# A graph layer's histogram and edge sums: one-hots with the chunk as the last index, and units of seven chunks

## The chip, the cores and the metric

The kernel runs on one core of a Trainium2 chip. Its five engines work side by side and meet through semaphores: PE (TensorE, matmuls and, as PEld, the loads of their weights), DVE (VectorE), ACT (ScalarE), POOL (GpSimd, which here issues gathers) and SP (SyncE, which issues the other transfers). The metric is the device time of one execution in microseconds.

## The reference

The input is a graph of N = 6250 nodes and E = 100000 edges, whose edges are sorted by destination, with a row of 512 numbers for each node. Four blocks follow one another, each added to its input:

```python
x = x + _L0_gnn_ref(_layernorm(x), node_vec1, W1, b1, gamma, beta, W2, b2, edge_index)   # A, B and part of C
x = x + _L0_ffn_ref(_layernorm(x)[None], w_gate, w_up, w_down)[0]                        # C
x = x + _L1_gnn_ref(_layernorm(x), edge_index, 6250, alpha, W, b)                        # D
x = x + _L1_ffn_ref(_layernorm(x)[None], switch_w, switch_b, expert_w, expert_b)[0]      # D and the last stage
...
deg = jax.ops.segment_sum(jnp.ones_like(src, dtype=x.dtype), dst, num_segments=N)   # first block, with self loops
h = x @ W1                                            # 512 -> 8
...
agg = jax.ops.segment_sum(x[src], dst, num_segments=num_nodes)                      # third block: rows of 512
agg = agg / jnp.maximum(deg, 1.0)[:, None]
return x + alpha * (agg @ W.T + b)
```

Two things matter here: the degree of each node, which is a histogram of the destinations, and the third block's sum of 512 numbers over the edges of each destination.

## The kernel before

The nodes lie in NT = 49 tiles of P = 128, the edges in C = 784 chunks of 128. The program has five stages, one behind the other, with a barrier of all engines between two: A (degrees and x @ W1), B (first edge sum and the quantized weights), C (second edge sum and the feed-forward block), D (third block and routing) and the experts. The change touches A and D, and one step of B.

**Stage A.** SP brings in the two edge lists and the rows of x. DVE turns the lists into numbers with an edge for each partition (`dstT`, `srcT`; PE does the transposes, DVE copies each of 14 blocks out of `pL`), finds for each chunk the first and the last tile and for each tile its range of chunks (lines 484 to 530, among them `pres`, `span`, `row` and `low_b`), and splits the destinations into `lo_f` (low 7 bits) and `hiT_f` (tile). Then a loop of G = 7 rounds runs on DVE, ACT and PE at once, each with its own order written out by hand:

- DVE: statistics of seven tiles of x (line 551), two histogram batches, the six small steps of the scales (`newton`, line 563), six more batches. A batch covers HU = 14 chunks: line 537 writes `ol`, 14 one-hots of 128 low ids, and line 540 `oh`, 14 one-hots of 49 tiles, each compared as f32 and written as bf16, laid out chunk by chunk. Two batches are buffered (`hist_used`).
- ACT: the scaled rows (`norm`, line 589) and the copies of the turned rows (line 603).
- PE: per batch 14 matmuls (line 653), with one chunk of `ol` as the 128 by 128 weights and the same chunk of `oh` as 49 columns, summed in `pD`; per tile four transposes (`turn`, line 636) and four matmuls with W1 (`layer1`, line 645), whose weights are the turned rows in f32.

The buffer `xt` of x holds one round, so the statistics of a round start when its loads are in. At the end DVE forms the degrees, `hid` and its split parts (lines 569 to 580), which SP stores.

**Stage D.** The chunks are grouped in CQ units of Q = 4. POOL gathers, chunk by chunk, rows of 1024 f16 numbers into a ring of RING = 7 units (line 1611). It waits for room in the ring (`rows_used`, counted up by DVE at line 1890) and, AHEAD = 3 units later, for the unit's arrival, which it passes on as `rows_ready` (line 1605). A unit is visited once for each tile that its edges reach. In a visit DVE builds the one-hots of the unit against that tile (line 1884, 512 numbers for each partition) and adds the sum of the visit before into `agg` (line 1872); PE multiplies each chunk's one-hot with both halves of its rows (line 1711, 2 Q matmuls of 512 columns) into one of two banks `pV`. Loops over units and visits have counts read from the tables `units` and `counts`, which stage B computes; at each unit's end PE and DVE read the next entry into a register. Behind a tile's units PE turns it (line 1728), multiplies it with W (1736, 1738) and computes the logits of a tile of the round before (1746, 1756). The rows of the tables are read at lines 1520 (`counts`) and 1523 (`units`).

## Time and profile before

| | us |
|---|---|
| median of three runs | 3950.85 |
| lowest and highest | 3946.94, 3951.02 |
| the profiled execution | 3950.55 |
| its span, first to last instruction | 3948.8 |
| stage A, up to the first work of stage B | 312.3 |
| its loop of seven rounds (43.0 to 293.5) | 250.5 |
| stage D, first gather to last (2417.7 to 3562) | about 1144 |

A timeline row gives the start, the duration, the engine, the line, the operation with its operands and how many instructions were merged; in brackets stands the idle time of the engine before it and what released it, where "issue" means that nothing in the profile was waited for. In a group's row the mean is that of one instruction.

### The profile page before, as it was taken

Reading aid. Unit: us, or ns where it says so; the run is one execution under the profiler, and the core shown is the slowest. Engines: PE = TensorE matmul, PEld = TensorE weight load, DVE = VectorE, ACT = ScalarE, POOL = GpSimd, SP = SyncE. Lnnn points to the kernel's source line nnn. Section 1 sums busy time; section 2 is a strip of 40 time slices with the busy share of each in tenths; the row PEclk is TensorE's granted clock in tenths of the full one; section 3 lists DMA queues with packets and bytes.
Section 4 is the critical chain, followed back from the end, with each engine's and each line's share of the span. In section 5 each row is a group of like instructions: output and inputs, shape, how many; then the busy total and the mean of one; then the engine's idle time right before and its main releaser. Section 6 shows DMA issues by size and latency. Waiting matters only on the chain. (4 is left out here: it accounts for less than half of the span.)

```text
span 3948.8 us, 60722 instructions
## 1 busy us (share of the span) xinstructions
PE 2807.3 (71%) x16139; PEld 2048.0 (52%) x16140; DVE 2086.5 (53%) x3745; ACT 1053.4 (27%) x1677; POOL 2087.1 (53%) x2184
## 2 busy tenths in 40 slices
PE   3664556320399999999999994677666676766599
PEld 3564555320277777777777883223232232323487
DVE  7777888992345454545454434443434434343476
ACT  1234446200123232323232331011111121213344
POOL 0006777775777777777500003776656665660254
PEclk9998778655599999999999997999999999997699
DMA  1113224102023333333322324777666666762464
GB/s 53 48 39 59 53 46 110 15 5 37 4 65 108 84 100 84 102 82 106 83 97 83 101 89 149 221 234 215 191 205 201 201 206 184 220 196 81 141 212 132
DMA packets 249317, 458.11 MB, mean 116 GB/s; under 512 B 93442, under 2 KB 115058, under 8 KB 249094
## 3 DMA queue, kind: packets, MB, share of 16 engines
q0 software_dynamic: 112384, 235.97, 23.1%
q1 hardware_dynamic: 136710, 219.40, 17.3%
q8 instruction: 111, 1.82, 0.2%
q14 instruction: 112, 0.92, 0.1%
HBM read 388.49 MB, written 73.25 MB: 117 GB/s over the span
## 5 line engine op out<-in xcount | busy, mean ns | idle before, releaser
L1611 POOL DMA_INDIRECT rows<-xn_rows,srcT x784 | 741.1, 945 | 403.6 <-issue 216.3
L115 POOL DMA_INDIRECT msg_c<-hid_rows,srcT x784 | 758.2, 967 | 251.2 <-issue 232.8
L1711 PE MATMUL pV<-rows,oh 128*128 x1952 | 474.1, 387 | 241.2 <-DVE agg L1872 193.8
L115 POOL DMA_INDIRECT msg_b<-hid_rows,srcT x464 | 455.7, 982 | 148.5 <-issue 137.2
L1711 PEld LDWEIGHTS pV<-rows,oh 128*128 x1952 | 190.6, 98 | 511.5 <-issue 356.9
L1273 PE MATMUL acc<-wd,hT 128*128 128x512 f32 x1617 | 414.8, 405 | 3.1 <-issue 1.2
L1248 PE MATMUL pG<-xT,wgu_hi 128*128 128x512 f32 (+1 forms) x1232 | 371.1, 382 | 22.9 <-issue 21.3
L1248 PE MATMUL pU<-xT,wgu_hi 128*128 128x512 f32 (+1 forms) x1232 | 364.2, 377 | 13.2 <-DVE sil L1417 13.2
L1884 DVE SCALAR_TENSOR_TENSOR oh<-ids,bases,dstT 128x512 f32 x244 | 183.2, 751 | 357.0 <-issue 322.7
L1273 PEld LDWEIGHTS acc<-wd,hT 128*128 128x128 f32 x1617 | 306.9, 193 | 77.4 <-issue 13.8
L1872 DVE TENSOR_TENSOR agg<-agg,pV x245 | 167.8, 685 | 269.2 <-PE pV L1711 257.8
L1248 PEld LDWEIGHTS pG<-xT,wgu_hi 128*128 128x128 f32 x1232 | 232.0, 193 | 67.6 <-issue 35.2
L1248 PEld LDWEIGHTS pU<-xT,wgu_hi 128*128 128x128 f32 x1232 | 230.3, 192 | 49.6 <-issue 22.3
L1038 PE MATMUL pG<-parts,los 128*128 128x200 bf16 x1920 | 220.9, 286 | 43.4 <-DVEq L874 24.7
L1597 POOL IOTA bases<- 128x49 f32 x1 | 0.2, 180 | 465.5 <-POOLq L334 465.5
L1736 PE MATMUL pW<-wgT,aT 128*128 128x512 f32 x392 | 211.2, 689 | 46.8 <-DVEq L1906 46.8
L1038 PEld LDWEIGHTS pG<-parts,los 128*128 128x128 bf16 x1920 | 201.5, 114 | 61.0 <-ACT los L1006 26.2
L1248 PE MATMUL pG<-xT,wgu_lo 128*128 128x512 f32 (+1 forms) x616 | 229.6, 373 | 0.0
L1248 PE MATMUL pU<-xT,wgu_lo 128*128 128x512 f32 (+1 forms) x616 | 228.7, 371 | 0.0
L1417 DVE TENSOR_TENSOR sil<-pU,sil 128x512 f32<-128x512 f32 (+1 forms) x154 | 95.8, 622 | 248.9 <-PE pU L1248 241.2
L1794 ACT ACTIVATE wg<-agg,invdeg 128x512 f32 (+1 forms) x49 | 35.3, 721 | 659.1 <-DVEq L104 659.1
L1325 ACT ACTIVATE sil<-pG 128x512 f32<-128x512 f32 (+1 forms) x154 | 84.0, 545 | 444.3 <-PE pG L1248 441.2
(362 smaller groups left out, 4625.9 us busy)
## 6 DMA issues: line engine op xcount, KB each, us to landing
wd<-wd_rows SPq DMA_DIRECT2D x154, 512.0 KB
we<-in_L_ffn_expert_w SPq DMA_DIRECT2D x16, 1024.0 KB, 8.0
msg_c<-hid_rows,srcT POOLq DMA_INDIRECT x784
x_rows<-xr SPq DMA_DIRECT2D x49, 256.0 KB, 4.1
xn_rows<-pair SPq DMA_DIRECT2D x49, 256.0 KB
rows<-xn_rows,srcT POOLq DMA_INDIRECT x784
res<-x_rows SPq DMA_DIRECT2D x49, 256.0 KB, 3.9
x_rows<-agg SPq DMA_DIRECT2D x49, 256.0 KB, 2.9
```

What stands on the lines that cost most here:

```text
L115: nc.gpsimd.indirect_dma_start(msg[:, c, :], None, table, bass.IndirectOffsetOnAxis(ap=srcT[:, c:c + 1], axis=0)).then_inc(landed[u % 2], 16)
L1038: last = nc.tensor.matmul(into, los[:, g % 2, b, k * P:(k + 1) * P], parts[:, j, b].rearrange("p f h -> p (f h)"), start=(b == 0 and j == ...
L1248: last = nc.tensor.matmul(ps[:, 0:n], w[:, c, :], v[:, c, :], start=(m == 0), stop=(m == len(terms) - 1))
L1273: last = nc.tensor.matmul(acc4[j][:], h, wd[:, slot, w, :], start=(f == 0 and m == 0), stop=(f == FB - 1 and m == 2))
L1325: nc.scalar.activation(sil[:, 0:n], pG[:, 0:n], ACT.Silu).then_inc(s["silu"], 1)
L1417: nc.vector.tensor_tensor(sil[:, 0:n], pU[:, 0:n], sil[:, 0:n], ALU.mult).then_inc(s["hmul"], 1)
L1611: nc.gpsimd.indirect_dma_start(rows[:, u % RING, c, :], None, xn2_rows, bass.IndirectOffsetOnAxis(ap=srcT[:, u * Q + c:u * Q + c + 1], axi ...
L1711: last = nc.tensor.matmul(pV[:, ds(to, 1), :].rearrange("p a d -> p (a d)"), oh[:, ds(of, 1), c, :].rearrange("p a d -> p (a d)"), rows[:, ...
L1736: nc.tensor.matmul(pW[:], aT[:, k % 2, c, :], wgT[:, c, :], start=(c == 0), stop=False)
L1794: nc.scalar.activation(scaled[:, k % 2, :], agg_at(T), ACT.Identity, scale=invdeg[:, ds(T, 1)]).then_inc(s["scaled"], 1)
L1872: nc.vector.tensor_tensor(at, at, pV[:, ds((v + 1) % 2, 1), :].rearrange("p a b -> p (a b)"), ALU.add).then_inc(s["added"], 1)
L1884: nc.vector.scalar_tensor_tensor(oh[:, ds(v % 4, 1)].rearrange("p a q n -> p (a q) n"), bc(ids.unsqueeze(1), (P, Q, P)), bases[:, ds(tile, ...
```

## The change

Constants: units of seven chunks in place of four, a ring of four units in place of seven (28 chunks both times), and the wait for a unit's arrival after the fourth gather of the unit behind it. Stage A: the lists are loaded in two parts, the first of which waits for nothing, and destinations first; `xt`, `var`, `mv` and `rs` are doubled; the one-hots are bf16 comparisons of a constant table `number` with `lo_b` and `hi_b`, four batches deep, laid out with the chunk as the last index; the list blocks are turned four and three at a time; and the rounds are written out, with the statistics and scales of the next round between the batches of this one, and the work on the tile ranges between the batches of the first. Stage B: the tile's last unit is found by a multiplication and a shift. Stage D: `landed` and `oh3` have two buffers each.

```diff
-Q = 4
+Q = 7
 CQ = C // Q
+BY_Q = -(-(1 << 16) // Q)
+assert CQ * Q == C and all(n * BY_Q >> 16 == n // Q for n in range(C))
...
-RING = 7
-BY_R = -(-(1 << 16) // 7)
+RING = 4
+BY_R = -(-(1 << 16) // RING)
 assert all(n * BY_R >> 16 == n // RING for n in range(256))
-AHEAD = 3
+LANDING = 4
...
-            ol = sb(ctx, "ol", [P, 2, HU, P], BF16)
-            oh = sb(ctx, "oh", [P, 2, HU, NT], BF16)
+            HB = 4
+            ol = sb(ctx, "ol", [P, HB, P, HU], BF16)
+            oh = sb(ctx, "oh", [P, HB, NT, HU], BF16)
+            number = sb(ctx, "number_a", [P, P, HU], BF16)
...
-                sp.dma_start(w1[:], W1.rearrange("(k p) h -> p k h", p=P)).then_inc(s["w1_in"], 16)
...
+                EA = 96
+                lists = ((dst, dst_em, "dst_in"), (src, src_em, "src_in"))
+                for lst, em, done in lists:
+                    sp.dma_start(em[0:EA, :], lst[0:EA * EB * P].rearrange("(p c) -> p c", p=EA)).then_inc(s[done], 16)
                 sp.wait_ge(s["cleared"], 2)
...
-                def load(i, k, rows=P):
-                    sp.dma_start(xt[0:rows, k, :], x[ds((i * G + k) * P, rows), :]).then_inc(x_in[k], 16)
+                def load(i, k):
+                    if i >= 2:
+                        sp.wait_ge(s["xT_ps"], (i - 2) * G + k + 1)
...
+                sp.dma_start(w1[:], W1.rearrange("(k p) h -> p k h", p=P)).then_inc(s["w1_in"], 16)
...
+                def histogram(i, m):
+                    n = i * HG + m
+                    if n >= HB:
+                        dve.wait_ge(s["hist_used"], n - HB + 1)
+                    nc.vector.tensor_tensor(ol[:, n % HB], number[:], bc(lo_b[:, n * HU:(n + 1) * HU].unsqueeze(1), (P, P, HU)),
+                                            ALU.is_equal).then_inc(s["ol"], 1)
+                    nc.vector.tensor_tensor(oh[:, n % HB], number[:, 0:NT], bc(hi_b[:, n * HU:(n + 1) * HU].unsqueeze(1), (P, NT, HU)),
+                                            ALU.is_equal).then_inc(s["oh"], 1)
...
+                first = {1: extreme_tiles, 2: lambda: turned_list(2), 3: lambda: turned_list(3), 4: spans, 6: span_rows, 7: tile_ranges}
...
+                nc.vector.memset(dst_em[96:EP, :], FAR).then_inc(s["cleared"], 1)
+                nc.vector.memset(src_em[96:EP, :], 0).then_inc(s["cleared"], 1)
...
-                def histogram(i, m):
-
-                    n, h = i * HG + m, m % 2
-
-                    dve.wait_ge(s["hist_used"], n + 1)
-                    nc.vector.tensor_tensor(
-                        ol[:, h, :, :], bc(iota[:].unsqueeze(1), (P, HU, P)),
-                        bc(lo_f[:, ds(n * HU, HU)].unsqueeze(2), (P, HU, P)), ALU.is_equal).then_inc(s["ol"], 1)
-                    nc.vector.tensor_tensor(
-                        oh[:, h, :, :], bc(iota[:, 0:NT].unsqueeze(1), (P, HU, NT)),
-                        bc(hiT_f[:, ds(n * HU, HU)].unsqueeze(2), (P, HU, NT)), ALU.is_equal).then_inc(s["oh"], 1)
...
-                with dve.Fori(0, G) as i:
-                    own.body(i, 3 + NEWTON)
-
-                    dve.wait_ge(s["xn"], i * G + G)
-                    for k in range(G):
-                        dve.wait_ge(x_in[k], (i + 1) * 16)
-                        last = nc.vector.bn_stats(st[:, k, :], xt[:, k, :])
-                    own.step(last)
...
-                    nc.vector.tensor_copy(sig[:, 0:1], var[:, 0:1]).then_inc(s["var"], 1)
-                    for m in range(2):
...
+                statistics(0, range(G))
+                variance(0)
+                for i in range(G):
+                    for m in range(HG):
                         histogram(i, m)
-                    dve.wait_ge(s["std"], i + 1)
-                    newton(nc, own, rs[:, :, 0], var[:], nw[:])
-                    nc.vector.scalar_tensor_tensor(rs[:, :, 1], mv[:, :, 0], -1.0, rs[:, :, 0],
-                                                   ALU.mult, ALU.mult).then_inc(s["stats"], 1)
-                    for m in range(2, HG):
-                        histogram(i, m)
-                own.end(G)
+                        if i == 0 and m == 0:
+                            scales(0)
+                        if i == 0 and m in first:
+                            first[m]()
+                        if i == 1 and m == 0:
+                            low_ids()
+                        if i + 1 < G:
+                            if m < 4:
+                                statistics(i + 1, range(2 * m, min(2 * m + 2, G)))
+                            if m == 4:
+                                variance(i + 1)
+                            if m == 6:
+                                scales(i + 1)
...
-                nc.vector.tensor_copy(sig[:, 0:1], degs[:, 0:1]).then_inc(s["degs"], 1)
...
-                own.step(nc.vector.tensor_scalar_max(invdeg[:], pD[:, 0:NT], 1.0))
-                own.step(nc.vector.reciprocal(invdeg[:], invdeg[:]))
-
-                dve.wait_ge(s["h_used"], G + 1)
+                dve.wait_ge(s["h_used"], G)
...
                 split3(nc, own, own3, hid, hrest)
                 dve.sem_inc(s["hid1"], 1)
+                own.step(nc.vector.tensor_scalar_max(invdeg[:], pD[:, 0:NT], 1.0))
+                own.step(nc.vector.reciprocal(invdeg[:], invdeg[:]))
...
                 def turn(i, k):
-                    pe.wait_ge(s["xn"], i * G + (k + G + 1))
+                    T = i * G + k
+                    pe.wait_ge(s["xn"], T + 1)
+                    if T >= 2:
+                        pe.wait_ge(s["xT"], T - 1)
                     for c in range(DK):
-                        last = nc.tensor.transpose(pT[k % 2][:, c * P:(c + 1) * P], xt[:, k, c * P:(c + 1) * P], ident[:])
+                        last = nc.tensor.transpose(pT[T % 2][:, c * P:(c + 1) * P], xt[:, i % 2, k, c * P:(c + 1) * P], ident[:])
                     last.then_inc(s["xT_ps"], 1)
 
...
                 def histogram(i, m):
-                    pe.wait_ge(s["ol"], i * HG + (m + 1))
-                    pe.wait_ge(s["oh"], i * HG + (m + 1))
+                    n = i * HG + m
+                    pe.wait_ge(s["ol"], n + 1)
+                    pe.wait_ge(s["oh"], n + 1)
                     for c in range(HU):
-                        last = nc.tensor.matmul(pD[:, 0:NT], ol[:, m % 2, c, :], oh[:, m % 2, c, :], start=False, stop=False)
+                        last = nc.tensor.matmul(pD[:, 0:NT], ol[:, n % HB, :, c], oh[:, n % HB, :, c], start=False, stop=False)
                     last.then_inc(s["hist_used"], 1)
 
-                with pe.Fori(0, G) as i:
-                    histogram(i, 0)
-                    histogram(i, 1)
-                    turn(i, 0)
-                    for k in range(G):
-                        if k + 1 < G:
-                            turn(i, k + 1)
-                        layer1(i, k)
-                        if k % 2 == 0:
-                            histogram(i, 2 + k // 2)
-                    for m in range(2 + -(-G // 2), HG):
+                for i in range(G):
+                    for m in range(HG):
                         histogram(i, m)
+                        if i == 0 and m in first:
+                            first[m]()
+                        if m < G:
+                            turn(i, m)
+                        if m > 0:
+                            layer1(i, m - 1)
                 nc.tensor.matmul(pD[:, 0:NT], identb[:], zeros[:], start=False, stop=True).then_inc(s["hist"], 1)
...
+                own.step(nc.vector.tensor_scalar_mul(v[1], v[1], float(BY_Q)))
                 own.step(nc.vector.tensor_copy(ti[0:1, 0, :], v[1]))
-                own.step(nc.vector.tensor_single_scalar(ti[0:1, 1, :], ti[0:1, 0, :], Q.bit_length() - 1, ALU.arith_shift_right))
+                own.step(nc.vector.tensor_single_scalar(ti[0:1, 1, :], ti[0:1, 0, :], 16, ALU.arith_shift_right))
...
-        landed = [sem(f"d_landed{h}") for h in range(AHEAD + 1)]
+        landed = [sem(f"d_landed{h}") for h in range(2)]
...
-            oh = sb(ctx, "oh3", [P, 4, Q, P], F16)
+            oh = sb(ctx, "oh3", [P, 2, Q, P], F16)
...
                 def arrived(u):
-                    pool.wait_ge(landed[u % (AHEAD + 1)], (u // (AHEAD + 1) + 1) * Q * 16)
+                    pool.wait_ge(landed[u % 2], (u // 2 + 1) * Q * 16)
                     pool.sem_inc(s["rows_ready"], 1)
 
...
-                    if u >= AHEAD:
-                        arrived(u - AHEAD)
-                for u in range(CQ - AHEAD, CQ):
-                    arrived(u)
+                            bass.IndirectOffsetOnAxis(ap=srcT[:, u * Q + c:u * Q + c + 1], axis=0)).then_inc(landed[u % 2], 16)
+                        if c + 1 == LANDING and u > 0:
+                            arrived(u - 1)
+                arrived(CQ - 1)
...
-                            to, of = v % 2, v % 4
+                            to = v % 2
...
-                                        oh[:, ds(of, 1), c, :].rearrange("p a d -> p (a d)"),
+                                        oh[:, ds(to, 1), c, :].rearrange("p a d -> p (a d)"),
...
-                            wait_alone(dve, s["mm_done"], v + 1, s["fence_dve"])
                             nc.vector.scalar_tensor_tensor(
-                                oh[:, ds(v % 4, 1)].rearrange("p a q n -> p (a q) n"), bc(ids.unsqueeze(1), (P, Q, P)), bases[:, ds(tile, 1)],
+                                oh[:, ds(v % 2, 1)].rearrange("p a q n -> p (a q) n"), bc(ids.unsqueeze(1), (P, Q, P)), bases[:, ds(tile, 1)],
```

PE, stage A, in one of the seven rounds; `pT` holds turned rows, `pH` the product with W1, `pD` the histogram. Before, the loop's start:

```order
L653 MATMUL pD<-oh,ol 128x49 x14
L650 REGISTER_ALU
L653 MATMUL pD<-oh,ol 128x49 x14
L634 ISA
L636 MATMUL pT<-ident,xt 128x128 x4
L634 REGISTER_ALU
L636 MATMUL pT<-ident,xt 128x128 x4
L642 REGISTER_ALU
L643 REGISTER_ALU
L645 MATMUL pH<-w,xT 128x8 x4
L650 REGISTER_ALU
```

Now, the second round:

```order
L709 MATMUL pD<-oh,ol 128x49 x14
L689 MATMUL pT<-ident,xt 128x128 x4
L709 MATMUL pD<-oh,ol 128x49 x14
L689 MATMUL pT<-ident,xt 128x128 x4
L700 MATMUL pH<-w,xT 128x8 x4
L709 MATMUL pD<-oh,ol 128x49 x14
L689 MATMUL pT<-ident,xt 128x128 x4
```

A batch of 14 stands ahead of each tile's transposes, and the product of a tile one batch behind its transposes, in place of two batches at the start and two or three at the end.

DVE, stage A, from the statistics of a round to its second batch. Before:

```order
L551 BN_STATS st<-xt 128x6 x7
L94 ISA
L555 BN_AGGR mv<-st 128x2 x7
L94 REGISTER_ALU
L557 TENSOR_SCALAR var<-mv 128x7
L94 REGISTER_ALU
L558 COPY sig<-var 128x1
L536 REGISTER_ALU
L537 ISA
L537 TENSOR_TENSOR ol<-iota,lo_f 128x1792
L540 REGISTER_ALU
L540 TENSOR_TENSOR oh<-iota,hiT_f 128x686
```

Now, in the second round:

```order
L492 BN_STATS st<-xt 128x6
L521 TENSOR_TENSOR ol<-number_a,lo_b 128x1792
L523 TENSOR_TENSOR oh<-number_a,hi_b 128x686
L499 BN_AGGR mv<-st 128x2 x7
L501 TENSOR_SCALAR var<-mv 128x7
L521 TENSOR_TENSOR ol<-number_a,lo_b 128x1792
L523 TENSOR_TENSOR oh<-number_a,hi_b 128x686
L521 TENSOR_TENSOR ol<-number_a,lo_b 128x1792
L523 TENSOR_TENSOR oh<-number_a,hi_b 128x686
L2219 RECIPROCAL rs<-rs 128x7
L2220 TENSOR_TENSOR nw<-var,rs 128x7
```

The statistics stand between the batches, two tiles at a time, and belong to the next round.

PE, stage D, the end of a unit: the last matmul, the two loop ends and the reading of the next unit. Before:

```order
L1711 ISA
L1711 MATMUL pV<-rows,oh 128x512
L1717 ISA
L1704 COMPARE_AND_BRANCH
L1718 ISA
L1523 TENSOR_LOAD units
L1523 ISA x2
L1688 ISA
L1698 COMPARE_AND_BRANCH
```

Now:

```order
L1764 ISA
L1764 MATMUL pV<-rows,oh 128x512
L1770 ISA
L1757 COMPARE_AND_BRANCH
L1771 ISA
L1577 TENSOR_LOAD units
L1577 ISA x2
L1741 ISA
L1751 COMPARE_AND_BRANCH
```

The same rows end a unit; ahead of them stand 14 matmuls in a visit in place of 8, each with one ISA row that sets an address.

## Rows read from the trace of the kernel before

**Rows 1.** window, then us and instructions of PE, PEld, DVE, ACT, POOL, clock, DMA.

```profile
43.00:293.50 250.50, 158.50 (x1358) 153.84 (x1358) 197.53 (x266) 74.07 (x118) 0.00 (x0) 1.00 0.15 45
...
2416.60:3562.00 1145.40, 768.08 (x3078) 342.77 (x3078) 482.66 (x853) 183.44 (x271) 741.74 (x788) 0.93 0.70 208
```

**Rows 2.** timeline of DVE, stage A: start, us, line, operation, idle before and its releaser.

```profile
18.72 0.63 DVE L481 CAST dst_f<-dst_em 112x896 f32<-112x896 int32 x1 [15.90 <-DMA dst_em<-in_dst]
...
19.80 0.62 DVE L484 TENSOR_SCALAR hi_i<-dst_em 112x896 int32<-112x896 int32 x1
...
27.79 1.02 DVE L504 CAST dstT<-pL 128x112 int16<-128x112 f32 x2
...
37.97 0.27 DVE L514 TENSOR_REDUCE spanr<-pL 98x1 f32<-98x112 f32 x1
...
42.92 4.25 DVE L551 BATCH_NORM_STATS2 st<-xt 128x6 f32<-128x512 f32 x7 [0.44 <-DVE low_b L530]
...
48.35 2.03 DVE L537 TENSOR_TENSOR ol<-iota,lo_f 128x1792 bf16<-128x1792 f32 x1
50.30 0.87 DVE L540 TENSOR_TENSOR oh<-iota,hiT_f 128x686 bf16<-128x686 f32 x1
51.08 2.02 DVE L537 TENSOR_TENSOR ol<-iota,lo_f 128x1792 bf16<-128x1792 f32 x1
```

**Rows 3.** timeline of PE, first round of stage A.

```profile
51.31 0.74 PE L653 MATMUL pD<-oh,ol 128*128 128x49 bf16 x14 [12.65 <-DVE oh L540]
...
59.43 0.75 PE L653 MATMUL pD<-oh,ol 128*128 128x49 bf16 x14
59.99 1.09 PE L636 MATMUL pT<-ident,xt 128*128 128x128 f32 x4
...
62.45 1.09 PE L636 MATMUL pT<-ident,xt 128*128 128x128 f32 x4
```

**Rows 4.** groups by line: operation, count | busy us, mean ns | idle us before, releasers.

```profile
L1711 PEld LDWEIGHTS pV<-rows,oh 128*128 x1952 | 190.6, 98 | 511.5 <-issue 356.9
...
L537 DVE TENSOR_TENSOR ol<-iota,lo_f 128x1792 bf16<-128x1792 f32 x56 | 113.3, 2023 | 50.3 <-PE pD L653 49.6
...
L645 PEld LDWEIGHTS pH<-w,xT 128*128 128x128 f32 x392 | 88.5, 333 | 1.5 <-ACT xT L603 1.5
...
L540 DVE TENSOR_TENSOR oh<-iota,hiT_f 128x686 bf16<-128x686 f32 x56 | 48.5, 867 | 0.0
...
L1962 DVE TENSOR_TENSOR names<-names,iota 128x448 bf16<-128x448 bf16 x7 | 4.4, 625 | 0.7
...
L1963 DVE TENSOR_SCALAR names<-names,lane 128x448 bf16<-128x448 bf16 x7 | 2.5, 352 | 0.2
```

**Rows 5.** timeline of DVE where the loop of stage A ends.

```profile
294.45 0.21 DVE L569 TENSOR_SCALAR degs<-pD 128x49 f32<-128x49 f32 x1 [0.97 <-PE pD L668]
```

**Rows 6.** timeline of PE, stage D, around one tile.

```profile
3002.64 1.90 PE L1711 MATMUL pV<-rows,oh 128*128 x8 [1.92 <-DVE agg L1872]
3006.25 1.90 PE L1711 MATMUL pV<-rows,oh 128*128 x8 [1.72 <-DVE agg L1872]
3008.54 1.90 PE L1711 MATMUL pV<-rows,oh 128*128 x8 [0.39 <-issue]
3012.11 0.63 PE L1728 MATMUL pT<-ident,wg 128*128 128x128 f32 x4 [1.67 <-issue]
```

**Rows 7.** timeline of PE, stage D, second visit of another tile.

```profile
3215.20 1.90 PE L1711 MATMUL pV<-rows,oh 128*128 x8 [0.91 <-issue]
```

**Rows 8.** timeline of DVE, stage D, beside Rows 6.

```profile
3003.89 0.75 DVE L1884 SCALAR_TENSOR_TENSOR oh<-ids,bases,dstT 128x512 f32 x1 [1.39 <-issue]
3005.07 0.69 DVE L1872 TENSOR_TENSOR agg<-agg,pV  x1 [0.43 <-issue]
```

**Rows 9.** gathers on POOL: the group, and one row of its timeline.

```profile
L1611 POOL DMA_INDIRECT rows<-xn_rows,srcT x784 | 741.1, 945 | 403.6 <-issue 216.3 <-DVEq L1890 186.4 <-DMA rows<-xn_rows,srcT 0.9
...
3013.41 0.94 POOL L1611 DMA_INDIRECT rows<-xn_rows,srcT  x1 [0.30 <-issue]
```

More of the change, by code:

```diff
@@ L374, in program @@
             "dve lists_f lists_ps lists_used lo_hi ol oh hist_used hist "
-            "span var std degs degs_std fence span_ps spanr row_ps ranges lows pool hid1 stored ".split())}
-        x_in = [sem(f"a_x_in{k}") for k in range(G)]
+            "span var std degs degs_std span_ps spanr row_ps ranges lows numbers pool hid1 stored ".split())}
+        x_in = [[sem(f"a_x_in{j}_{k}") for k in range(G)] for j in range(2)]
         with ExitStack() as ctx:
@@ L472, in _ @@
                 nc.gpsimd.memset(dstT[:, C:DX], FAR).then_inc(s["const"], 1)
+                nc.gpsimd.iota(number[:], [[1, P], [0, HU]], base=0, channel_multiplier=0,
+                               allow_small_or_imprecise_dtypes=True).then_inc(s["numbers"], 1)
             @block.vector
@@ L476, in _, with statistics @@
                 own = Steps(dve, s["dve"])
-                nc.vector.memset(src_em[:], 0).then_inc(s["cleared"], 1)
-                nc.vector.memset(dst_em[:], FAR).then_inc(s["cleared"], 1)
-                dve.wait_ge(s["dst_in"], 32)
+                def statistics(i, ks):
+                    for k in ks:
+                        dve.wait_ge(x_in[i % 2][k], (i // 2 + 1) * 16)
+                        last = nc.vector.bn_stats(st[:, k, :], xt[:, i % 2, k, :])
+                    own.step(last)
@@ L501, in _ @@
[L501 to L506 removed]
+                turned_list(0)
+                turned_list(1)
+                dve.wait_ge(s["lists_used"], 2)
@@ new lines, in turn_list, with spans @@
+                    last.then_inc(s["lists_ps"], 1)
+                for j in range(4):
+                    turn_list(j) if j < 2 else None
+                nc.tensor.matmul(pD[:, 0:NT], identb[:], zeros[:], start=True, stop=False)
+                def spans():
+                    pe.wait_ge(s["span"], 1)
+                    pe.wait_ge(s["lists_used"], 4)
+                    nc.tensor.transpose(pL[0][0:2 * NT, 0:EP], span[:].rearrange("p a b -> p (a b)"),
+                                        ident[0:EP, 0:EP]).then_inc(s["span_ps"], 1)
```

212 lines of the change are left out of this document (118 added, 94 removed).

## The prediction

> **What bounds the kernel now.** I read the windows by stage first, then the timelines of two stages. A barrier stands between the stages, so that a microsecond saved in a stage is saved in the whole, and only A and D change much. The loop of stage A takes 250.5 us, and no engine is busy for all of it: DVE for 197.5 and PE for 158.5 [rows 1]. The reader is to see why in the timelines: each round begins with the statistics of seven tiles, in which PE has nothing to do, and later DVE waits for one of its two buffers, which PE frees late (50.3 us over the loop, [rows 4]). A round takes 250.5 / 7 = 35.8 us. Before it stand 42.9 us in which DVE prepares the lists [rows 2]. The granted clock is 1.00 in the loop, which is the level of 2.4 GHz.
>
> Stage D could be taken as bound by its gathers. POOL starts one every 1.25 us (0.94 us and 0.30 before it, [rows 9]), which for 784 is 980 us of 1145. But POOL also stands 186.4 us behind DVEq L1890, the count that frees the ring [rows 9]: it is held back by the consumers. Of these PE is the later one. Its visits last 1.90 us. From a unit's last visit to the next start 3.61 us pass, inside a unit 3.61 - 1.71 + 0.39 = 2.29 [rows 6]. The gap of 1.7 us is attributed to `agg`, but the same 1.67 stands before the transposes at L1728, which don't read `agg` and whose releaser is "issue" [rows 6]. So it belongs to the end of a unit: loop ends and the load of the next table entry. The table load and the branches are rows of the program's order that don't change.
>
> **Stage A, start.** The first batch reaches PE at 51.3 us [rows 3]. Of DVE's work ahead of it these leave: the first and last tiles and their spans, 27.79 - 19.80 = 8.0 us; the tile ranges and low ids, 42.92 - 37.97 = 5.0 us [rows 2]. They come back in the first round (12 us) and the second (about 1 us). Of the 14 list copies, 10.2 us from 27.79 to 37.97 with the five conversions, the seven of src move too and the other seven become two; I put list and conversions at 2.5 + 3.0 us, an estimate from the five conversions in those 10.2 us and the copies' rows. The destinations arrived at 18.7 us, last in their queue; now they are first, and most of the list doesn't wait for the memsets. If that brings nothing, PE starts at 18.7 + 1.2 (casts) + 5.5 + 5.4 (statistics, from 42.92 to 48.35) + 1.4 = 32.2 us; if it brings 9 us, at 23. I take 28.
>
> **Stage A, DVE's round.** One batch costs DVE 1.95 us for `ol` and 0.78 for `oh`, start to start [rows 2]. The difference of 1.17 us for 1106 numbers is 1.06 ns each, with 0.05 us fixed. All operands are now bf16 and dense. The case shows no such comparison: a bf16 multiplication with one f32 operand, 625 ns for 448 numbers, has no gain; with no f32 stream, 352 ns, it does [rows 4]. So the new cost lies between nothing gained (2.73 us a batch) and half for each number (1.00 + 0.42 = 1.42). I take 1.42, since the second row differs from the first in just what the change makes different. The Trainium skill, "VectorE: DVE Perf Modes", section "The perf-mode tier table", gives two-operand bf16 instructions in SBUF twice the rate; no row of this case shows it for two streams. A round is then 8 x 1.42 + 5.4 (statistics) + 1.2 (six small steps of about 0.2, as in [rows 5]) = 18.0 us, against 28.4 without the gain.
>
> **Stage A, PE's round.** A tile's four transposes and four products take 62.45 - 59.99 = 2.46 us; a batch of 14 takes 59.99 - 59.43 = 0.56 us, or 40 ns a matmul [rows 3]. The four buffers and the statistics of the next round ahead of time let PE go on from batch to tile, and ACT's copies and scalings have the whole round for seven tiles, so that nothing but PE's own work is on the path. At the old price a round is 7 x 2.46 + 8 x 0.56 = 21.7 us. But PE now reads both operands with a step of 14 numbers, 28 bytes. No row shows a strided read. The lower end is 40 ns. The upper end is the nearest row of a slow weight load, f32 weights at 333 ns each [rows 4]: 7 x 2.46 + 112 x 0.333 = 54.5 us. Between them lies a bf16 load that nothing overlaps, 98 ns on average at L1711 [rows 4], and I take this, 112 x 0.098 + 17.2 = 28.2 us: if reads get slower, the overlap that makes 98 ns into 40 is what goes first.
>
> The Trainium skill has a rule on either side. "SBUF — State Buffer", section "Door 1: The DMA port swizzle", says that reads run at full rate while successive accesses fall on the same line of 16 bytes, and pay for each new line; by it every one of these reads pays, which speaks against the change. "TensorE: Matmul & The Clock Gate", section "Weight-path perf modes — Fast Weight Load (FWL) and DoubleRow", keeps the fast load for 128 bf16 weights at such a step. By the second the round would be the 21.7 us of the rival below, by the first alone more. No run here shows either yet.
>
> **Stage A, sum.** The first round has DVE's 18.0 + 12.4 = 30.4 us, more than PE's 28.2; six rounds follow at 28.2: 28 + 30.4 + 169.2 = 227.6 us. Before, the loop ended at 293.5 (PE's last matmul released DVE at 294.45, [rows 5]). Saved: 65.9, and 0.9 more since the two `invdeg` steps move behind `hid1`, behind which SP's store and the barrier wait. That is 67. The iota of `number` on POOL (1792 numbers for each partition) is over long before 20 us. SP's loads wait for a tile of two rounds earlier and have no one behind them who is late.
>
> **Stage B.** One small step more, and about a dozen on a row of 162 in place of 246: nothing, within 1 us. They stand on DVE ahead of the tiles' loop.
>
> **Stage D.** From the inputs: 196 units and 244 visits become 112 units and, with 48 tile borders, 160 visits; matmuls rise from 1952 to 2240. A visit of 14 at 1.90 / 8 = 0.2375 us is 3.33 us. Before: 196 x 3.61 + 48 x 2.29 = 817 us. Now, if the gap at a unit's end stays: 112 x (3.33 + 1.71) + 48 x (3.33 + 0.39) = 743 us. Saved: 74. The gap may also shrink: where PE's sequencer had run ahead it was 0.91 [rows 7], and longer matmuls hide more of the issue. Then DVE's chain bounds a unit: sum of the visit before (0.53 us after its end, 0.69 long), 1.39 of issue, the one-hot at 0.75 + 384 x 1.04 ns = 1.15, and some 0.7 to PE's start, 4.5 to 4.6 us [rows 6, 8]. 112 x 4.6 + 48 x 3.5 = 683 us would save 134. I take 74, since three of four gaps at a unit's end in [rows 6, 7] are the long ones. DVE's added 0.4 us in a visit lies beside 3.33 us of PE, its summations fall by 84 beside PE as well; the removed wait on `mm_done` had been met two visits before.
>
> The ring holds 28 chunks as before, but is freed by the unit: POOL may run some 14 to 21 chunks ahead instead of 20 to 24. With 1145 - 74 = 1071 us for 980 us of gathers that should do. A unit is announced four gathers, 5 us, behind its last one instead of 15.
>
> **The sum.** 3950.55 - 67 - 74 = 3809.6 us, against the profiled execution's own time, which is 0.3 us below the median of the three runs.
>
> **Rivals.** (1) *Strided reads cost nothing*: a round of 21.7, A saves 105 + 1, 3950.55 - 106 - 74 = 3770 us. For it: weights go in faster than numbers one by one already. (2) *Strided reads are the new bound, and slower*: at the f32 price the loop ends at 28 + 7 x 54.5 = 410 us, A loses 115, 3950.55 + 115 - 74 = 3992 us. It decides from 28 + 7 x (17.2 + 112 p) = 368, p = 0.28 us a matmul. For it: each column is its own access for both operands. Against it: that is seven times the dense price. (3) *Stage D gains nothing*: with two units ready, a tile's 8 us of other work, or the ten-us stall of POOL once a round, empties the ring, or landing takes over 5 us; 3950.55 - 67 = 3884 us. (4) *The comparisons don't speed up*: DVE's 28.4 us bound the round, first round 40.8, end at 29 + 40.8 + 170.4 = 240, A saves 54, 3823 us.
>
> **How the numbers follow.** Forecast 0.40, rival 1 0.34, rival 2 0.07, rival 3 0.12, rival 4 0.07. The predicted time is the forecast's, 3810 us. The range goes down to rival 1 with D's better bound, 3950.55 - 106 - 130 = 3715, and up to rival 3, 3885; rival 2 stays out. A measurement of this kernel can tell about 0.2%. Faster by more 0.92, within it 0.01, slower 0.07.
>
> **What would show it.** Right: line 521 near 1.05 us; the first PE batch before 33 us; a batch of 14 in about 1.4 us, rounds of 28 us without idle time on PE; in D units 5.0 us apart, POOL's wait for the ring down to about 110 us. Wrong: a batch of 14 on PE at 0.6 us or at 4; PE waiting for POOLq in D; line 521 still at 2.0 us.

## The result, and the profile after

The changed kernel takes 3727.68 us, the median of four runs (3721.67 to 3729.46), against 3950.85 before: a ratio of 0.9435, with an interval of 0.9418 to 0.9451. Its profiled execution has a span of 3726.1 us, 222.7 us less than before. Of the kernels below, `d_alone` had one run of four at a lower granted clock, 4492.61 us at 0.653 in place of 0.89, which its numbers leave out. By stage, from the first gather of one to that of the next:

| us | before | after | saved | forecast |
|---|---|---|---|---|
| A, up to B's first gather | 313.5 | 242.3 | 71.2 | 67 |
| B | 628.7 | 626.6 | 2.1 | 0 |
| C | 1475.5 | 1466.3 | 9.2 | 0 |
| D, first gather to the last matmul of the sums | 1173.6 | 1039.9 | 133.7 | 74 |
| D, from there to the experts' first matmul | 118.5 | 112.6 | 5.9 | 0 |
| experts | 239.0 | 238.4 | 0.6 | 0 |

The windows of stages A and D after, in the columns of [rows 1]:

```profile
23.70:223.30 199.60, 194.35 (x1382) 193.00 (x1382) 130.93 (x268) 65.62 (x111) 0.00 (x0) 1.00 0.16 48
2334.00:3360.00 1026.00, 821.46 (x3394) 375.50 (x3394) 434.54 (x696) 184.19 (x272) 743.56 (x788) 0.92 0.77 232
```

In A, PE is busy for 194 of 199.6 us, where it was for 158 of 250; DVE has time to spare. In D the clock and the gathers' count are as before, in 1026 us instead of 1145.

Stage A starts earlier. The timeline of DVE, which stands beside [rows 2]:

```profile
22.06 1.09 DVE L521 TENSOR_TENSOR ol<-number_a,lo_b 128x1792 bf16<-128x1792 bf16 x1
23.07 0.51 DVE L523 TENSOR_TENSOR oh<-number_a,hi_b 128x686 bf16<-128x686 bf16 x1
23.50 0.20 DVE L2219 RECIPROCAL rs<-rs 128x7 f32<-128x7 f32 x1
```

`ol` costs 1.01 us and `oh` 0.43, start to start, in place of 1.95 and 0.78. PE's first batch starts at 23.73 us in place of 51.3. PE in the second round, beside [rows 3]:

```profile
64.57 1.48 PE L709 MATMUL pD<-oh,ol 128*128 128x49 bf16 x14
65.88 1.05 PE L689 MATMUL pT<-ident,xt 128*128 128x128 f32 x4
66.72 1.72 PE L700 MATMUL pH<-w,xT 128*128 128x8 f32 x8
68.29 1.48 PE L709 MATMUL pD<-oh,ol 128*128 128x49 bf16 x14
```

From 61 us on no idle time is left, a tile's transposes and products take 68.29 - 65.88 = 2.41 us (2.46 before), and a batch of 14 takes 65.88 - 64.57 = 1.31 us (1.29 to 1.32 elsewhere) in place of 0.56. Stage D around three tiles, beside [rows 6]:

```profile
2908.55 3.19 PE L1764 MATMUL pV<-rows,oh 128*128 x14
2912.57 6.27 PE L1764 MATMUL pV<-rows,oh 128*128 x28 [0.83 <-issue]
2920.10 0.63 PE L1781 MATMUL pT<-ident,wg 128*128 128x128 f32 x4 [1.27 <-issue]
...
2949.96 3.19 PE L1764 MATMUL pV<-rows,oh 128*128 x14 [0.67 <-issue]
2954.44 5.84 PE L1764 MATMUL pV<-rows,oh 128*128 x26 [1.29 <-DVE agg L1925]
```

Visits of 14 matmuls take 3.19 us, and the gaps between units 0.67 to 1.29 us instead of 1.7. A unit whose edges reach two tiles is visited twice, and these two visits follow each other with no gap (28 matmuls in one row, cut at 26 by the window's edge in the last). The groups of D's sums and of its gathers, beside [rows 4, 9]:

```profile
L1665 POOL DMA_INDIRECT rows<-xn_rows,srcT x784 | 743.2, 948 | 282.2 <-issue 244.4 <-DVEq L1942 23.6 <-DMA rows<-xn_rows,srcT 14.2
L1764 PE MATMUL pV<-rows,oh 128*128 x2240 | 528.8, 392 | 94.5 <-issue 44.9 <-DVE agg L1925 38.9 <-DVE oh L1936 10.3
```

POOL waits 23.6 us for room in the ring, where it waited 186.4; 743.2 + 282.2 us cover the stage, and 244.4 of the idle time is "issue", most of it the 0.30 us between two gathers: issuing the gathers is now nearly all of it.

### The profile page after: what moved, and what is told of

Its sections match the earlier page's. It is cut to its first block and busy times, and to the rows that moved or that the text cites. A ratio compares the mean times of both kernels' runs of the same rounds, so it can differ in the third digit from the quotient of the medians.

```text
span 3726.1 us, 57890 instructions
## 1 busy us (share of the span) xinstructions
PE 2878.9 (77%) x16427; PEld 2109.9 (57%) x16428; DVE 1957.7 (53%) x3559; ACT 1045.3 (28%) x1671; POOL 2091.5 (56%) x2185
## 5 line engine op out<-in xcount | busy, mean ns | idle before, releaser
L1665 POOL DMA_INDIRECT rows<-xn_rows,srcT x784 | 743.2, 948 | 282.2 <-issue 244.4
L1764 PE MATMUL pV<-rows,oh 128*128 x2240 | 528.8, 392 | 94.5 <-issue 44.9
L1764 PEld LDWEIGHTS pV<-rows,oh 128*128 x2240 | 223.2, 100 | 387.7 <-issue 180.1
L1936 DVE SCALAR_TENSOR_TENSOR oh<-ids,bases,dstT 128x896 f32 x160 | 184.1, 1151 | 210.7 <-issue 210.5
L1925 DVE TENSOR_TENSOR agg<-agg,pV x161 | 110.1, 684 | 336.6 <-PE pV L1764 335.2
L1386 ACT CAST hT<-sil 128x512 fp32r<-128x512 f32 (+1 forms) x154 | 87.3, 567 | 405.9 <-DVE sil L1471 404.6
```

The lines of the kernel that those rows point to most:

```text
L1386: nc.scalar.copy(hT[:, slot, 0, 0:n], sil[:, 0:n]).then_inc(s["h_hi"], 1)
L1665: nc.gpsimd.indirect_dma_start(rows[:, u % RING, c, :], None, xn2_rows, bass.IndirectOffsetOnAxis(ap=srcT[:, u * Q + c:u * Q + c + 1], axi ...
L1764: last = nc.tensor.matmul(pV[:, ds(to, 1), :].rearrange("p a d -> p (a d)"), oh[:, ds(to, 1), c, :].rearrange("p a d -> p (a d)"), rows[:, ...
L1925: nc.vector.tensor_tensor(at, at, pV[:, ds((v + 1) % 2, 1), :].rearrange("p a b -> p (a b)"), ALU.add).then_inc(s["added"], 1)
L1936: nc.vector.scalar_tensor_tensor(oh[:, ds(v % 2, 1)].rearrange("p a q n -> p (a q) n"), bc(ids.unsqueeze(1), (P, Q, P)), bases[:, ds(tile, ...
```

## Experiments

Six kernels change the one-hots of stage A, three change D (two of them were run twice), and one changes only the length of PE's program. Each is quoted with what was written before it ran.

**The stages apart.** `d_only` takes the parts of B and D into the kernel before, as in the diff ahead; `d_q4` takes units of four into the kernel after:

```diff
-Q = 7
+Q = 4
...
-RING = 4
+RING = 7
```

> The kernel before with the changes of stages B and D alone (units of seven, ring of four, arrival after the fourth gather, two one-hot buffers, no wait on mm_done); stage A stays as before. From the profile after: first gather of stage D to its last matmul 1039.9 us against 1173.6 before, and 5.9 us less from there to the experts. Theory (the stages' gains are separate, and D gives 134 to 140 us): 3950.9 - 140 = 3811 us, stage A up to the first gather of stage B 313 us as before. Rival (stage C's 9.2 us, which came for no reason that the change shows, hang on the layout of memory that stage D's smaller tables bring): 3802, with stage C at 1466 in place of 1475 us. Second rival (D gained because stage A left something different): D above 1060, over 3835 us.

> The kernel after with units of four and a ring of seven again, all else kept (arrival passed on after the fourth gather of the next unit, two one-hot buffers, no wait on mm_done in DVE). Theory (what was gained in D is the fixed price of a unit's end on PE, which 84 units fewer don't pay and longer visits hide): D back at 1165 to 1185 us from first gather to last matmul, gaps of 1.6 to 1.8 us between the visits of two units, total 3727.7 + 135 = 3863 us (3845 to 3880). Rival (the removed wait of DVE or the earlier announcement did it): D below 1100, total under 3790 us.

Both told nothing about D: where they ran, every kernel was slow, and the kernel before took 5713 us. `d_only` took 5660 us and `d_q4` 5640. The gathers of D in `d_only`:

```profile
L1614 POOL DMA_INDIRECT rows<-xn_rows,srcT x784 | 746.5, 952 | 656.2 <-DVEq L1891 410.8 <-issue 227.8 <-DMA rows<-xn_rows,srcT 17.5
```

POOL waits 410.8 us for the ring, so it is held back by the consumers. They hardly wait for the gathers: the time that PE and its weight loads stood idle at D's sums is put to "issue" for 812.1 us (854 times; in the kernel after 225.0, 279 times) and to the units' arrival for 10.1. The expectation of `d_q4_again` below blames the gathers, which these numbers don't bear out; what slowed these kernels stays open. Stage A, which has no gathers, took 313.5 us in `d_only` and 241.9 in `d_q4`, as expected. The same two kernels ran again, beside a kernel before of 3949.9 us:

> The same kernel as d_only (before, with the changes of stages B and D alone). Theory (the stages are separate): first gather to last matmul 1040 us, total 3951 - 134 - 6 = 3811 us. If stage C's 9 us come with the tables of stage D: 3802.

`d_alone` took 3807.7 us, the median of three (ratio 0.9652, 0.9633 to 0.9671), with 1037.9 us from first gather to last matmul and stage C at 1475.0. The stages are separate, and C's 9 us don't come from D.

> The same kernel as d_q4 (after, with units of four and a ring of seven). In the first comparison every kernel's gathers were slow, the kernel before's too, so that stage D stood on them in all kernels. Where gathers take 1.25 us each again: theory (the fixed price of a unit's end on PE): first gather to last matmul 1165 to 1185 us, total 3863 us (3845 to 3880). Rival (DVE's removed wait or the earlier announcement brought it): under 1100 us, total under 3790.

`d_q4_again` took 3856.8 us (0.9767, 0.9751 to 0.9783), with 1174.8 us in D, what the kernel before has. All that D gained comes from the size of the unit; with units of four, the removed wait of DVE, the two buffers and the earlier announcement bring nothing that can be seen. PE in it, in the columns of [rows 6]:

```profile
2918.72 1.90 PE L1764 MATMUL pV<-rows,oh 128*128 x8 [1.68 <-DVE agg L1925]
2920.91 1.90 PE L1764 MATMUL pV<-rows,oh 128*128 x8 [0.29 <-issue]
2924.49 0.63 PE L1781 MATMUL pT<-ident,wg 128*128 128x128 f32 x4 [1.68 <-issue]
```

The gap behind a unit is 1.68 us again. It stands before a visit and before the transposes alike.

**What the gap is.** `d_split` leaves the columns as they are and doubles the instructions:

```diff
-for m in range(2):
+for m in range(4):
...
-pV[:, ds(to, 1), :].rearrange("p a d -> p (a d)"),
+pV[:, ds(to, 1), m % 2 * 256:m % 2 * 256 + 256].rearrange("p a d -> p (a d)"),
...
-rows[:, ds(at, 1), c, m * D:(m + 1) * D].rearrange("p a d -> p (a d)"),
-start=(c == 0 and m == 0), stop=(c == Q - 1 and m == 1))
+rows[:, ds(at, 1), c, m * 256:m * 256 + 256].rearrange("p a d -> p (a d)"),
+start=(c == 0 and m == 0), stop=(c == Q - 1 and m == 3))
```

> The kernel after with each matmul of stage D's sums of 512 columns issued as two of 256: 28 instructions a visit in place of 14, the same columns. Theory (PE's sequencer bounds a unit: from consecutive visits of two units, 3.61 us with 8 matmuls and 4.48 with 14, each matmul costs it 0.145 us and a unit's end 2.45): a unit takes 2.45 + 28 x 0.145 = 6.5 us in place of 4.5, and a visit inside a unit 4.1 + 0.6 = 4.7; stage D's sums 112 x 6.5 + 48 x 4.7 = 954 us with about 340 us of other work on PE, first gather to last matmul near 1300 us. Rival (the gap at a unit's end is a fixed wait behind the array's last matmul, whatever the count of instructions): 1040 to 1070 us.

Measured: 1249.8 us in D, 3952.4 in all (3941.2 to 3963.4). The rival falls. PE's timeline:

```profile
2904.42 3.22 PE L1764 MATMUL pV<-rows,oh 128*128 x28
2908.99 3.95 PE L1764 MATMUL pV<-rows,oh 128*128 x28 [1.35 <-DVE agg L1925]
2913.92 3.97 PE L1764 MATMUL pV<-rows,oh 128*128 x28 [0.98 <-issue]
2920.18 0.73 PE L1781 MATMUL pT<-ident,wg 128*128 128x128 f32 x4 [2.30 <-issue]
```

The first visit behind other work takes 3.22 us, near the 3.19 of 14 matmuls: its 28 instructions had been handed over while the tile's other work ran, and neither they nor their weight loads take the array longer than that. The next take 3.95 and 3.97 us, 0.141 us an instruction, and the gap at the unit's end grows to 2.30. So PE's sequencer (the part of PE that reads the program and hands the instructions to the array) hands out a matmul of the sums in 0.141 us, and a unit's end costs it about 3.61 - 8 x 0.141 = 2.5 us. Its own rows show this directly. In the kernel after they follow one another from 2951.86 us, when the last matmul of a visit has been handed out, to the next visit's first matmul at 2954.43: 2.57 us of register steps, two branches, a table load and three semaphore waits, none of which blocks. Two of the groups, in the window from 2951.8 to 2954.5 us:

```profile
L1577 PEldq TENSOR_LOAD <-units x1: 307/307/307, 2952.3 to 2952.3; - x1
L106 PEldq EVENT_SEMAPHORE  x3: 51/51/51, 2953.4 to 2953.9; - x3
```

The array needs 0.228 us for a matmul of 512 columns. A visit of 8 lets the sequencer gain 8 x 0.087 = 0.7 us on it, a visit of 14 gains 1.2, and a tile's other work gains more; what is left of the 2.5 is the gap. The 1300 us expected were 50 too many; some 35 of them, an estimate, are the first visits behind a tile's other work, 48 times 3.95 - 3.22 us, which are not slowed.

**Stage A: type or layout.** `a_dense` lays both one-hots out chunk by chunk as before, still in bf16; `a_f32` keeps the layout and widens the operands:

```diff
-ol = sb(ctx, "ol", [P, HB, P, HU], BF16)
+ol = sb(ctx, "ol", [P, HB, HU, P], BF16)
...
-nc.vector.tensor_tensor(ol[:, n % HB], number[:], bc(lo_b[:, n * HU:(n + 1) * HU].unsqueeze(1), (P, P, HU)),
-                        ALU.is_equal).then_inc(s["ol"], 1)
...
+nc.vector.tensor_tensor(ol[:, n % HB], bc(row_b[:].unsqueeze(1), (P, HU, P)),
+                        bc(lo_b[:, n * HU:(n + 1) * HU].unsqueeze(2), (P, HU, P)), ALU.is_equal).then_inc(s["ol"], 1)
...
```

```diff
-lo_b = sb(ctx, "lo_b", [P, C], BF16)
-hi_b = sb(ctx, "hi_b", [P, C], BF16)
+lo_b = sb(ctx, "lo_b", [P, C], F32)
+hi_b = sb(ctx, "hi_b", [P, C], F32)
...
-number = sb(ctx, "number_a", [P, P, HU], BF16)
+number = sb(ctx, "number_a", [P, P, HU], F32)
```

> The kernel after with the one-hots laid out chunk by chunk as before (PE reads both operands dense), still compared as bf16 numbers, lo_b and hi_b now constant along the innermost index. Theory (PE's 1.30 us for a batch of 14 is the price of the step of 28 bytes, and DVE needs both operands dense to double its rate): batch on PE 0.56 us, ol 2.0 us and oh 0.85 us on DVE as before, which then bounds the round at 8 x 2.73 + 5.4 + 1.2 = 28.4 us against 27.3 now; total 3727.7 + 7 x 1.1 to 2 = 3736 to 3745 us. Rival (bf16 alone gives DVE its rate): ol near 1.1 us, PE's round 21.7 us, total 3727.7 - 7 x 5.6 = 3689 us. Second rival (the 1.30 us have another cause than the step): batch stays at 1.30 us.

> The kernel after with number_a, lo_b and hi_b in f32, layout unchanged (chunk as the last index, PE reads with the step of 28 bytes). Theory (DVE's doubling comes from all operands being 2 bytes wide): ol 2.0 us, oh 0.85 us, PE's batch still 1.30 us; DVE's round 28.4 us bounds, and the first round 12 us more: total 3727.7 + 7 x 1.1 + 4 + 6 = 3740 to 3755 us. Rival (the order of the loops did it, not the type): ol near 1.1 us, total as after, 3728 us.

These two ran beside `d_only`, so only stage A is read: 253.1 us for `a_dense`, 258.8 for `a_f32`, against 241.9 for `d_q4` with the stage A of after. The groups, first of `a_dense`, then of `a_f32`:

```profile
L523 DVE TENSOR_TENSOR ol<-row_b,lo_b 128x1792 bf16<-128x1792 bf16 x56 | 113.3, 2024 | 2.0
...
L711 PE MATMUL pD<-oh,ol 128*128 128x49 bf16 x784 | 41.6, 217 | 57.1 <-DVE oh L525 57.1
```

```profile
L521 DVE TENSOR_TENSOR ol<-number_a,lo_b 128x1792 bf16<-128x1792 f32 x56 | 113.3, 2023 | 2.0
...
L709 PE MATMUL pD<-oh,ol 128*128 128x49 bf16 x784 | 83.2, 274 | 28.5 <-DVE oh L523 28.5
```

`ol` costs 2024 ns with bf16 numbers of which one is constant along the innermost index, 2023 with f32 and the new layout, and 1090 only with both. In `a_dense` PE's matmuls are dense and a batch of 14 takes 0.56 to 0.57 us again, so the 1.30 are the price of the step. `a_dense` also shows where A's 71 us come from: it reaches 253.1 us with the new order and the old prices, so that order and start bring 60 us of them and the new one-hots 11.

**Which operand's step.** `a_oh_dense` makes only `oh` dense for PE, `a_ol_dense` only `ol`, each with the lines of `a_dense` for that tile.

> The kernel after with only oh (the 49 columns that pass through PE) laid out chunk by chunk and compared against a constant along the innermost index; ol, PE's weights, keeps the step of 28 bytes. Theory (the weights' step is what costs: each weight load reads 128 columns, the moving side only 49): batch on PE stays at 1.2 to 1.30 us, oh on DVE 0.87 us, stage A 242 plus or minus 2, since DVE's round grows only to 8 x (1.00 + 0.78) + 6.6 = 20.8 us. Rival (the moving side's step costs it): batch 0.56 us, PE's round 21.7 us, stage A 205 us.

> The counterpart: ol (weights) laid out chunk by chunk, oh (49 columns) keeps the chunk as the last index. DVE: ol 2.02 us, oh 0.51 us, round 8 x (1.95 + 0.42) + 6.6 = 25.6 us. Theory (the weights' step costs): batch on PE 0.56 to 0.7 us, PE's round 21.7 to 22.7 us, DVE bounds at 25.6: stage A 7 x 1.7 = 12 us less on the rounds and some 3 us more in the first, 231 to 237 us. Rival (the moving side's step costs): batch 1.2 to 1.3 us, stage A at 242 or above.

PE's timelines, of `a_oh_dense` and of `a_ol_dense`:

```profile
103.61 1.01 PE L711 MATMUL pD<-oh,ol 128*128 128x49 bf16 x14
104.44 1.09 PE L691 MATMUL pT<-ident,xt 128*128 128x128 f32 x4
```

```profile
103.20 1.43 PE L711 MATMUL pD<-oh,ol 128*128 128x49 bf16 x14
104.45 1.05 PE L691 MATMUL pT<-ident,xt 128*128 128x128 f32 x4
```

My theory, that the weights' step is what costs, was wrong. With the step on the weights alone a batch takes 0.83 us, 59 ns a matmul; with the step on the 49 moving columns alone it takes 1.25 us, 89 ns, nearly the 93 of both. The moving side pays 1.8 ns a column in place of 0.8. Stage A took 224.6 and 248.1 us, the whole kernels 3709.5 and 3733.1.

**How long a step.** `a_pair` makes the chunk the last index only within pairs of chunks, `a_seven` within sevens:

```diff
-ol = sb(ctx, "ol", [P, HB, P, HU], BF16)
+HK = 2
+ol = sb(ctx, "ol", [P, HB, HU // HK, P, HK], BF16)
...
-last = nc.tensor.matmul(pD[:, 0:NT], ol[:, n % HB, :, c], oh[:, n % HB, :, c], start=False, stop=False)
+last = nc.tensor.matmul(pD[:, 0:NT], ol[:, n % HB, c // HK, :, c % HK], oh[:, n % HB, c // HK, :, c % HK], start=False, stop=False)
```

> The kernel after with the chunk as the last index only within pairs of chunks: ol is laid out as 7 pairs x 128 rows x 2, so PE reads both operands with a step of 4 bytes in place of 28, and DVE's innermost dense run is 2 numbers long in place of 14; number_a shrinks to 128 x 2. Theory 1 (a weight or column read slows PE from 40 to 93 ns a matmul only where the step passes some size below 28 bytes, and DVE needs only that the innermost step is one number): batch on PE 0.56 us, ol 1.0 to 1.2 us; PE's round 21.7 us, stage A 7 x 5.2 to 5.6 = 37 to 39 us shorter than after's 242.3, 204 us. Theory 2 (any step costs PE the same): batch 1.30 us, stage A 242. Theory 3 (DVE pays for short dense runs): ol near 2.0 us, round 28.4 us on DVE, stage A 250 to 255.

> As a_pair, but the chunk is the last index within groups of seven, a step of 14 bytes for PE. a_pair's batch of 14 took 0.57 to 0.61 us with a step of 4 bytes, after's 1.30 with 28. Theory (the price begins with the step that leaves a piece of memory of 16 bytes; Trainium skill, 'SBUF - State Buffer', section 'Door 1: The DMA port swizzle', names such lines): at 14 bytes nearly every read is a new line, so the batch costs 1.1 to 1.3 us, stage A 235 to 242 us. Rival (two one-byte-doubled numbers of a word, or a step up to 16 bytes, are free): 0.6 us, stage A 198 us.

`a_pair` took 3676.6 us (3668.5 to 3683.0; ratio to before 0.9304, 0.9283 to 0.9325), 51 us less than the changed kernel, with stage A at 197.5. It beats both kernels. Some 9 of the 44.8 us that stage A gains on the kernel after come from PE's rate and not from the layout: one round of its profile, from the batch at 99.48 us to that at 112.92, takes 13.4 us, where the one before takes 21.9 (last section). Its comparison of `ol` costs the same 1090 ns, and PE pays nearly nothing for a step of 4 bytes. PE's timeline; its first two rows give the price, the others are for the last section:

```profile
99.48 0.75 PE L711 MATMUL pD<-oh,ol 128*128 128x49 bf16 x14
100.04 1.09 PE L691 MATMUL pT<-ident,xt 128*128 128x128 f32 x4
...
103.33 0.53 PE L711 MATMUL pD<-oh,ol 128*128 128x49 bf16 x14
103.70 0.64 PE L691 MATMUL pT<-ident,xt 128*128 128x128 f32 x4
104.18 0.96 PE L702 MATMUL pH<-w,xT 128*128 128x8 f32 x8
```

100.04 - 99.48 = 0.56 us for 14 matmuls, as dense. `a_seven` took 3713.5 us, stage A 233.1:

```profile
63.65 1.30 PE L711 MATMUL pD<-oh,ol 128*128 128x49 bf16 x14
64.77 1.06 PE L691 MATMUL pT<-ident,xt 128*128 128x128 f32 x4
```

1.12 us a batch, 80 ns a matmul, with a step of 14 bytes; `ol` costs 1224 ns there. So the price comes between 4 and 14 bytes, and is mostly there at 14; a step of 8 bytes was not run, and whether the length of the step or the odd count of numbers makes it isn't shown. The Trainium skill, "SBUF — State Buffer", section "Door 1: The DMA port swizzle", tells of lines of 16 bytes that successive accesses should stay on: the three batches, 0.56, 1.12 and 1.30 us, rise with the share of reads that meet a new line (a quarter, seven eighths, all), as that rule has it. The 8 numbers of bf16 that the same section gives as a step for free don't hold here: at 7 numbers a matmul costs 80 ns in place of 40.

**Stage C.** Its 9 us are in every kernel with the new stage A and in none without: 1463.7 to 1468.1 us in seven profiles against 1475.5 and 1475.0 in two.

```diff
-                with pe.Fori(0, G) as i:
+                for i in range(G):
                     histogram(i, 0)
```

> The kernel before with one edit: stage A's loop of seven rounds is written out on PE alone (65 rows more in PE's program); DVE, ACT, SP and all of stages B to D as before. Open is why stage C takes 1466 us in every kernel with the new stage A and 1475 in the two without: PE waits 22.0 us on nothing that the profile shows ahead of the gate's matmuls there (8 times, up to 3.4 us) against 7.3 us (4 times). Theory (it hangs on where stage C's code lies in PE's program, which stage A's length shifts): stage C changes by more than 3 us, to 1466 or to another value, and the 22.0 us with it. Rival (it hangs on the memory or the data that stage A leaves): stage C 1475, the 22.0 us unchanged. On stage A itself: theory (its rounds are bound by the order of the work, statistics first, and two buffers, not by PE's loop): rounds of 35.8 us, stage A 313 us, within 1 us. Rival (the loop's branches on PE cost): 35.8 less 0.3 to 1 us a round, 306 to 311.

`pe_unrolled` took 3939.4 us (0.9976, 0.9967 to 0.9986), with stage C at 1464.9 and stage A at 314.2. PE's waits in the middle 1000 us of stage C, in total, times, and the longest, of `pe_unrolled`, before and after:

```profile
PE pG L1248 <- issue: 8.8, 5, 2.6
```

```profile
PE pG L1248 <- issue: 21.3, 8, 2.9
```

```profile
PE pG L1302 <- issue: 9.7, 4, 3.7
```

With 65 more rows ahead of it in PE's program, the same code of stage C waits 8.8 us in place of 21.3 for nothing that the profile names. The memory and the data that stage A leaves are those of before, so the rival falls. The whole kernel gains 7.8 us between the medians, a little less than the 10.6 us of stage C in one profile of each. How the length of the program acts stays open. From D's last matmul to the experts the same kernel has 113.0 us, `d_alone` 113.9, and only the profile of before 118.5: the 5.9 us there aren't shown to be of any change.

## Why the prediction was right, and where it was wrong

The range of 3715 to 3885 held the time, and the direction was right; the predicted 3810 was 82 us too slow. The step that failed is the size of D's term: 74 us with the gap at a unit's end kept at 1.71 us, where the runs showed 133.7. In A the sum is right to 4 us, partly by luck: two of its prices were read from rows that don't carry them.

- **Stage D**: the prediction took 74 us since the gap at a unit's end would stay at 1.71 us. PE's idle time ahead of the visits and of a tile's transposes fell from 241.2 + 75.2 = 316.4 us to 94.5 + 48.0 = 142.5, by 173.9; the working has it fall from 196 x 1.71 + 48 x 0.39 = 354 to 112 x 1.71 + 48 x 0.39 = 210, by 144. It named the reason why it could be less ("longer matmuls hide more of the issue") and kept the better bound, 134, for the range; the measured 133.7 meets that bound by chance, since DVE's chain wasn't the limit. PE's visits cost less than thought too, 528.8 - 474.1 = 54.7 us more busy time for 288 matmuls and not 69. The 30 us of idle time and the 14 of visits make 44 of the 60 us that D's term was short; the rest lies in PE's other work on the tiles. Counting which gaps of [rows 6, 7] were long was the wrong way to choose: they were long because the visits ahead of them were short. The rows gave the sum, 3.61 us from unit to unit with 1.9 of array time in it, but not how it splits between the matmuls and the unit's end; the expectation of `d_split` split it, and its run bore that out.
- **Stage D, gathers**: forecast a wait for the ring of 110 us, measured 23.6. POOL's 1024.3 us from first to last gather are 44 above the 980 that 784 gathers take; the next thing to be had there is the gather itself.
- **Stage A, start**: forecast 28 us with 23 as the better end, measured 23.7.
- **Stage A, DVE**: forecast 1.42 us a batch, measured 1.44. The choice was right, but its ground was thin: the two cited rows (625 and 352 ns) differ in more than the type, since the fast one has one stream and a number for each partition, and the slow one a second stream that is constant along the innermost index, which, as `a_dense` shows, is enough to lose the gain. The Trainium skill's "VectorE: DVE Perf Modes", section "The perf-mode tier table", gives two-operand bf16 instructions twice the rate, and the trace agrees where both bf16 operands are dense: 1090 ns against 2023.
- **Stage A, PE**: forecast 98 ns a matmul, measured 93; from PE's start to the loop's end 199.6 us, forecast 199.6. That is luck twice over. The 98 ns are how long a load's row lasts in stage D, where PE runs at twice the rate (last section) and the loads lie beside matmuls; in stage A before, such a row lasted 119 ns (its median) though a matmul cost 40. The reason was wrong too: not an uncovered weight load, but 49 moving columns at 1.8 ns. And the equal sums hide that the first round was longer than forecast, 33.9 us and not 30.4, and from the third on the rounds were shorter, 27.4 and not 28.2. The fast weight load, which the Trainium skill's "TensorE: Matmul & The Clock Gate", section "Weight-path perf modes — Fast Weight Load (FWL) and DoubleRow", keeps at such a step, doesn't keep the matmul at its dense price: 59 ns with the step on the weights alone, against 40. Rival 1 (reads with a step for nothing) fell at 28 bytes and holds at 4.
- **Stage A, clock**: the prediction reads a granted clock of 1.00 in the loop as 2.4 GHz. PE worked there at half of its rate (last section). Apart from the 98 ns this cost nothing, since the other prices of A are rows of A.
- **Stages B, C, experts, and from D to the experts**: 0 was forecast; 18 us came. For the 9.2 of stage C `pe_unrolled` shows that lengthening PE's program ahead of it is enough (10.6 there). None of the rows that the prediction cites points at it.
- Terms and their errors: A 4, D 60, the rest 18, together 82 us.

## What to carry to other kernels

A gap behind short loops on PE can be the sequencer's own time: compare the gap behind long and short visits, and if it shrinks, try a longer visit before touching semaphores. A layout that suits one engine has a price on the other, and the price hangs on the step in bytes: pairs (4 bytes) gave DVE its double rate and PE its dense rate, where 28 bytes cost PE 53 ns a matmul, at the lower level of its clock. After a change that moves code, a stage that wasn't touched may differ too: stage C did by 9.2 us, 0.6% of it.

## What was not expected of the hardware

- DVE's comparison of 1792 numbers takes 1090 ns with all three operands bf16 and dense in runs of 2 or 14, 1224 in runs of 7 (an odd count), and 2023 where one is f32 or constant along the innermost index.
- A step costs TensorE more on the moving side: 49 columns at 28 bytes 89 ns, 128 by 128 weights at 28 bytes 59 ns, both dense 40 ns. All of them are taken at the lower level of PE's clock; what they are at the higher isn't shown.
- In stage A, PE works at half of its rate, though the windows print a clock of 1.00: four transposes take 0.85 to 0.89 us there and 0.47 in stage D. The trace holds no record of the clock before 253.2 us in the kernel after, nor before 102.6 us in `a_pair`, and the 1.00 is what a window prints where it has none. The first record of `a_pair` grants 1.00 from 102.6 to 112.9 us, and just there the rate doubles (rows above: 0.37 us for the batch and 0.48 for the transposes); the next grants 0.50, the level of 1.2 GHz, and the rate falls back. Both rise once more from 116.3 to 119.7 us and then stay down to the end of the stage:

```profile
43.00:103.00 60.00, 57.72 (x520) 57.22 (x518) 56.30 (x123) 24.80 (x43) 0.00 (x0) 1.00 0.26 79
103.00:112.00 9.00, 9.00 (x150) 9.00 (x149) 7.68 (x20) 7.26 (x13) 0.00 (x0) 1.00 0.59 157
112.00:180.00 68.00, 65.20 (x603) 64.60 (x599) 46.70 (x93) 27.39 (x48) 0.00 (x0) 0.53 0.12 34
```

  PE had no idle time there from 57 us until the rate rose, and none until it fell; in the kernel after it had none from 61 to 223 us, and its rate never rose, so what lifts it is not shown. A printed clock of 1.00 (2.4 GHz) is thus no proof that PE runs at it. Compare the time of one kind of instruction at two places, and take a stage's prices from rows of that stage.
